# Four layers in one kernel: TensorE's work of a pair put in another order, SyncE's queries and masks issued first

## The chip, the cores and the metric

One core of a Trainium2 chip runs the whole program. The metric is device time in microseconds from launch to end. Three runs of the kernel before took 1097.38, 1100.94 and 1102.38 us. TensorE (PE) multiplies and transposes into PSUM, VectorE (DVE) and ScalarE (ACT) read PSUM and write SBUF, GpSimd (POOL) issues gathers, SyncE (SP) issues the other DMAs.

## The reference, cut to what matters

`x` is 64 sequences of 64 tokens of 512 values. Four layers, each added to its input:

```python
x = x + einsum('bct,bcd->bdt', x, W0[cond])                    # L0: a 64x64 matrix per sequence
q, k, v = x @ Wq.T, x @ Wk.T, x @ Wv.T                         # L1: 8 heads, 4 groups, 64 wide
q, k = rope(rms(q)), rope(rms(k))                              #     k, v scattered into 16-token blocks
p = softmax(where(allowed, q @ k_all.T / 16, -inf))            #     window of 256 keys before each token
x = x + (p @ v_all) @ Wo.T
x = x + einsum('bsi,bio->bso', x, W2[id]) + b2[id]             # L2: one of 16 experts (1 MB) per sequence
x = x + x @ W3.T + s * ((x @ A[ad].T) @ B[ad].T)               # L3: a shared matrix and a rank-16 adapter
```

## The kernel before

Two sequences make a pair: 128 tokens fill the 128 partitions, and there are 32 pairs. Stage A (the first 290 us or so) does L0, the projections, norm and rotation, and leaves x, queries and new keys and values in DRAM. Stage B, from about 290 us on, is what the change touches. Each engine runs its own instruction stream through the pairs: four written out, a loop of two pairs a turn, then the last ones. In turn `p` the attention of pair `p` runs, the output projection and the expert of pair `q = p - 1`, and the last layer of pair `r = p - 2`.

The attention of a pair has four steps `j`, two for each sequence, each with two units `u = 2j` and `2j + 1` that alternate between two buffers:
- GpSimd gathers 336 old rows of keys and values of a sequence into KV (`held`) and overwrites the new ones (`fresh`). `held(b)` of pair p waits until `values` of the same sequence of pair p - 2 is done (L1130).
- `keys` on TensorE turns the keys into bank 4 (L1418), ScalarE copies them to KT.
- `scores` (L1431): two products of 64 rows by 128 columns, one in each half of the array's rows, 336 columns each, into banks 0 and 1. They wait for KT, for the queries QB (first step), and for the earlier maxima `s_mx`, after which the banks are free.
- `masked` on VectorE (L1309) adds the mask FM and takes the maximum, `exp` on ScalarE (L1240) makes the probabilities and their sum, `norm` on VectorE (L1317, L1320) scales them.
- `turn` on TensorE (L1439) transposes them, `probs` on ScalarE copies them to PT, `values` on TensorE (L1452) multiplies them with the values: products 64 columns wide, one in each half of the array's columns, into bank 5. `heads` splits the result into high and low parts (OTH, OTL).

The rest of a turn: `output` (12 products over L93, the full array, bank 7), the sum x2 on VectorE (L1377), `turn_x(XB2)` (L1408), a copy to XT2, `expert` (L1477: 8 products of 64 columns, bank 6), the sum x3 (L1331), `turn_x(XB3)`, high and low parts XTH3 and XTL3, `adapter` (12 products of 128 columns), `dense3` (12 products of 512) and `adapted_sum`, and the last sum `out_sum` (L1337). Products in float32r are made exact by three (`exact_products`, L87 to L93), which is why each matrix comes as high and low.

Nothing plans the order: each `body` is written out by hand, with semaphores between engines, and an engine that waits holds all that stands behind. TensorE's is at L1523 to L1591, ScalarE's at L1254, VectorE's at L1339. SyncE's turn (L1184 to L1223) issues, in order: the expert weights of the first sequence (`weights(0)`, after `s_l2` of pair p - 2 and after the gather `held(1)` of pair p + 1 landed), the store of pair p - 2, x of pair p (after the sum x2 of pair p - 1), queries and masks of pair p + 1, the bias rows, and the weights of the second sequence (after `held(0)` of pair p + 2 landed).

Of the kernel before, what the change touches and what calls it, by code (L numbers as in the profile page):

```python
# [96 lines left out]
def build(nc, t, out):  # L97
    ctx = ExitStack()
    with ctx:
# [914 lines left out]
        with pb:  # L1014
# [148 lines left out]
            def _(sp):  # L1163
# [20 lines left out]
                def body(pr, attention, dense, adapted):  # L1184
# [22 lines left out]
                    if isinstance(p, int) and p == 0:  # L1207
                        sp.wait_ge(s_new[1], 16 * NCH)
                    if attention:
                        weights(0)  # L1210
# [6 lines left out]
                    if isinstance(p, int) and p == 0:  # L1217
                        sp.wait_ge(s_qto, 16 * PAIRS)
                    if not last_pair(pr):
                        queries(pr.move(1))  # L1220
                        windows(pr.move(1))
# [7 lines left out]
            def _(act):  # L1229
# [24 lines left out]
                def body(pr, attention, dense, adapted):  # L1254
                    p, q, r = pr.n, pr.n - 1, pr.n - 2
                    if adapted:
                        act.wait_ge(s_x3p, at(r, 1, 0))
                        copy(XTH3[:, :, :].rearrange("p k t -> p (k t)"), bank[7][:, :]).then_inc(s_xt3h, 1)
                    if dense:
                        probs(q, 6)  # L1260
                        probs(q, 7)
                    if attention:
                        exp(p, 0)
                        exp(p, 1)
                    if dense:
                        heads(q, 1)
                    if attention:
                        keys(pr, 1, 0)

                        probs(p, 0)  # L1270
                        probs(p, 1)
                        exp(p, 2)
                        exp(p, 3)

                        probs(p, 2)
                        probs(p, 3)
                        exp(p, 4)
                        exp(p, 5)
                        keys(pr, 1, 1)
                        heads(p, 0)  # L1280
                    if dense:
                        act.wait_ge(s_x2p, at(q, 1, 0))
                        copy(XT2[:, :, :, :].rearrange("p k b t -> p (k b t)"), bank[7][:, :]).then_inc(s_xt2, 1)

                    if attention:
                        probs(p, 4)
                        probs(p, 5)
                        exp(p, 6)
                        exp(p, 7)
                        if not last_pair(pr):  # L1290
                            keys(pr.move(1), 0, 0)
                            keys(pr.move(1), 0, 1)

                keys(Pair(0, 0), 0, 0)
                keys(Pair(0, 0), 0, 1)
# [3 lines left out]
            def _(dve):  # L1299
# [39 lines left out]
                def body(pr, attention, dense, adapted):  # L1339
# [23 lines left out]
                    if attention:  # L1363
                        masked(pr, 2)
                        masked(pr, 3)
                    if attention:
                        norm(p, 1)
                    if adapted and not last_dense(p):
                        out_sum(r, 6)
# [4 lines left out]
                    if dense:  # L1374
                        dve.wait_ge(s_o, at(q, 1, 0))
                        dve.wait_ge(s_x1in, at(q, 16, 15))
                        v.tensor_tensor(XB2[:, :], bank[7][:, :], XB1[:, :], ALU.add).then_inc(s_x2, 1)  # L1377
                    if attention:
                        norm(p, 2)
                        heads(p, 0)  # L1380
# [9 lines left out]
                    if attention:  # L1390
                        masked(pr, 6)
                        masked(pr, 7)
                        norm(p, 3)
                    if dense:
                        dve.wait_ge(s_xbb, at(q, 1, 0))
                        x3(q)

# [3 lines left out]
            def _(pe):  # L1401
# [10 lines left out]
                def keys(pr, b, gp):  # L1412

                    k = 2 * pr.par + b
                    if gp == 0:
# [106 lines left out]

                def body(pr, attention, dense, adapted):  # L1523
# [15 lines left out]
                    if attention:  # L1539
                        pe.wait_ge(s_kt, at(p, 4, 1))  # L1540
                        keys(pr, 1, 0)
                    if dense:
                        values(before, 3)
                    if adapted:
                        adapter(r, 7)
                        dense3(0, 2, True)

                    if attention:
                        scores(pr, 1)
                        turn(p, 0)  # L1550
                        turn(p, 1)
                    if adapted:
                        dense3(2, KC, False)
                        adapted_sum(r, 6)
                    if attention:
                        values(pr, 0)
                    if dense:
                        if adapted:
                            pe.wait_ge(s_xam, at(r, 1, 0))
                        output(q, 0, 2)  # L1560

                    if attention:
                        scores(pr, 2)
                        turn(p, 2)
                        turn(p, 3)
                    if dense:
                        output(q, 2, KC)
                    if attention:
                        values(pr, 1)
                        pe.wait_ge(s_kt, at(p, 4, 2))  # L1570
                        keys(pr, 1, 1)
                    if dense:
                        pe.wait_ge(s_x2, at(q, 1, 0))
                        turn_x(XB2, s_x2p)

# [4 lines left out]
                    if dense:  # L1580
                        expert(before, 0, 2)
                    if attention:
                        values(pr, 2)
                    if more:
                        pe.wait_ge(s_kt, at(p, 4, 3))
# [3 lines left out]
                    if more:  # L1589
                        pe.wait_ge(s_kt, at(p + 1, 4, 0))  # L1590
                        keys(pr.move(1), 0, 1)  # L1591

                keys(Pair(0, 0), 0, 0)
                pe.wait_ge(s_kt, 1)
                keys(Pair(0, 0), 0, 1)
# [51 lines left out]
```

## Time and profile before

| | |
|---|---|
| median of three runs | 1100.94 us |
| the profiled execution | 1101.85 us |
| its span, first to last instruction | 1100.0 us |
| mean granted TensorE clock | 0.984 |
| PE busy | 1031.8 us, 94% |
| DVE, ACT, POOL busy | 60%, 49%, 49% |
| DMA, mean over the span | 178 GB/s in packets |

In the timelines, "idle before" stands in brackets with what ended it. A row "x4" merges four instructions that lie together: its start is that of the first, its length reaches to the modelled end of the last. Matmuls are pipelined, so the step from one start to the next is what one costs, and is shorter than its length. PE and PEld are matmuls and weight loads; the sizes behind a tile's name, as 64*128, are the rows and columns of the array in use. In a row of sums (a stretch, its length, the busy time of PE, PEld, DVE, ACT and POOL with counts) the last three numbers are the granted clock, the DMA engines' share and GB/s.

### The profile page before, as it was taken

The numbers are of one execution on the slowest core, as the hardware profiler recorded it, in microseconds if no ns is written. First come the engines' busy times: TensorE is split into PE (matmuls) and PEld (weight loads), VectorE is DVE, ScalarE is ACT, GpSimd is POOL, SyncE is SP. The second block draws the span as 40 slices with busy tenths as digits, with TensorE's granted clock in tenths as the row PEclk, the third lists the DMA queues.
The fourth block names the chain that finished last, engine by engine and source line by source line (L and its number), as shares of the span: only waits on it lengthen the run. The fifth ranks groups of instructions, "written<-read, shape, count | busy, mean of one in ns | idle before, by whom it ended". The sixth has DMA issues, their size and how long they took to land.

```text
span 1100.0 us, 24023 instructions
## 1 busy us (share of the span) xinstructions
PE 1031.8 (94%) x6438; PEld 699.2 (64%) x6438; DVE 658.4 (60%) x1928; ACT 534.8 (49%) x1337; POOL 535.1 (49%) x597
## 2 busy tenths in 40 slices
PE   8999999999459999999999999999999999999998
PEld 6767777677336666666666666666666666666665
DVE  5889897567435555555555555555555555555552
ACT  4457776575344444444444444444444454444441
POOL 3555455257565455545544545555455545554400
PEclk9999999999689999999999999999999999999999
DMA  4433533454366666666666666666666666666631
GB/s 134 134 132 119 172 123 125 145 192 162 105 184 201 215 207 200 191 216 189 185 215 199 207 198 206 197 193 184 219 200 205 192 212 192 187 195 215 204 127 53
DMA packets 95337, 196.16 MB, mean 178 GB/s; under 512 B 31346, under 2 KB 40114, under 8 KB 87110
## 3 DMA queue, kind: packets, MB, share of 16 engines
q1 hardware_dynamic: 63942, 149.49, 41.7%
q0 software_dynamic: 30784, 44.16, 14.7%
q10 hardware_dynamic: 576, 2.10, 0.5%
q8 instruction: 15, 0.25, 0.1%
q14 instruction: 20, 0.16, 0.0%
HBM read 195.08 MB, written 33.56 MB: 208 GB/s over the span
## 4 chain that ended last, share of the span: by engine, by line
PE 64%; ACT 3%; issue 3%; DMA 2%; POOL 1%; ACTq 0%; DVE 0%; SPq 0%; POOLq 0%; DVEq 0%
PE bank L93 23%; PE bank L1477 10%; PE bank L1452 9%; PE bank L1431 9%; PE bank L1439 7%; PE bank L1418 4%; ACT PT L1231 2%; PE bank L1408 2%; DMA QB<-qt_scratch 2%; ACT KT L1231 1%; POOL KV L1132 0%; DMA KV<-in_pool,idxs 0%; POOL KVE L1142 0%; ACTq L76 0%; PE bank L1498 0%
## 5 line engine op out<-in xcount | busy, mean ns | idle before, releaser
L1231 ACT ACTIVATE PT<-bank 112x384 f32<-112x384 f32 x256 | 111.8, 489 | 263.2 <-PE bank L1439 263.0
L1309 DVE CUSTOM_DVE_ANT_0 SM<-bank,FM 128x336 f32<-128x336 f32 x256 | 129.8, 507 | 171.4 <-PE bank L1431 147.6
L1132 POOL DMA_INDIRECT KV<-in_pool,idxs x96 | 95.4, 993 | 116.5 <-PE bank L1452 94.9
L1132 POOL DMA_INDIRECT KVE<-in_pool,idxs_e x90 | 90.6, 1007 | 121.0 <-PE bank L1452 101.1
L1240 ACT ACTIVATE PR<-SM,nb 128x336 f32<-128x336 f32 x256 | 145.9, 577 | 1.7 <-DVE nb L1313 1.5
L1142 POOL DMA_INDIRECT KV<-kv_scratch,idxs x96 | 96.3, 1004 | 62.6 <-DMA KV<-in_pool,idxs 35.7
L1431 PE MATMUL bank<-KT,QB 64*128 64x336 f32 x512 | 108.9, 503 | 16.0 <-DMA QB<-qt_scratch 10.3
L1477 PE MATMUL bank<-W,XT 128*64 128x512 f32 x512 | 123.7, 604 | 0.0
L1142 POOL DMA_INDIRECT KVE<-kv_scratch,idxs_e x93 | 92.7, 997 | 62.7 <-DMA KVE<-in_pool,idxs_e 32.4
L1231 ACT ACTIVATE KT<-bank 128x336 f32<-128x336 f32 x128 | 57.5, 450 | 132.1 <-PE bank L1418 130.1
L93 PE MATMUL bank<-wqh,XTH 128*128 128x512 f32 x256 | 105.8, 413 | 9.6 <-DVE XTL L500 6.5
L1439 PEld LDWEIGHTS bank<-ident,PR 128*112 128x112 f32 x768 | 82.4, 134 | 46.3 <-issue 44.6
L1439 PE MATMUL bank<-ident,PR 128*112 128x128 f32 x768 | 110.7, 281 | 0.1
L93 PE MATMUL bank<-wqh,XTL 128*128 128x512 f32 x256 | 101.3, 396 | 0.0
L93 PE MATMUL bank<-wql,XTH 128*128 128x512 f32 x256 | 101.2, 395 | 0.0
L1320 DVE TENSOR_SCALAR PR<-PR,rinv 128x336 f32<-128x336 f32 x256 | 90.4, 395 | 4.5
L780 POOL TENSOR_TENSOR RT<-RT,SW 128x384 f32<-128x384 f32 x31 | 31.4, 1013 | 120.9 <-DVE SW L509 120.9
L1431 PEld LDWEIGHTS bank<-KT,QB 64*128 64x128 f32 x512 | 39.3, 187 | 51.0 <-issue 33.4
L93 PEld LDWEIGHTS bank<-wqh,XTH 128*128 128x128 f32 x256 | 48.7, 190 | 26.9 <-DVE XTL L500 13.9
L1331 DVE TENSOR_TENSOR XB<-bank,XBB 128x512 f32<-128x512 f32 x32 | 22.1, 692 | 71.9 <-PE bank L1477 71.9
L1452 PE MATMUL bank<-PT,KVE 112*64 112x128 f32 x768 | 55.8, 281 | 9.4 <-ACT PT L1231 9.4
L1317 DVE RECIPROCAL rinv<-rs 128x2 f32<-128x2 f32 x128 | 20.9, 163 | 72.1 <-ACT PR L1240 72.1
(195 smaller groups left out, 2175.0 us busy)
## 6 DMA issues: line engine op xcount, KB each, us to landing
W<-in_w SPq DMA_DIRECT2D x64, 1024.0 KB, 5.8
FM<-mask SPq DMA_DIRECT2D x64, 168.0 KB, 3.9
X<-in_x SPq DMA_DIRECT2D x32, 256.0 KB, 2.8
x_scratch<-X SPq DMA_DIRECT2D x32, 256.0 KB, 2.0
qt_scratch<-QT SPq DMA_DIRECT2D x32, 256.0 KB, 2.9
QB<-qt_scratch SPq DMA_DIRECT2D x32, 256.0 KB, 2.9
XB<-x_scratch SPq DMA_DIRECT2D x32, 256.0 KB
BB<-in_b SPq DMA_DIRECT2D x64, 128.0 KB
```

The source lines that it names most:

```text
L93: last = mm(out, l, r, start=start and i == 0, stop=stop and i == len(todo) - 1)
L1132: pool.indirect_dma_start(out=KV[k][:, c, :], out_offset=None, in_=t["pool"], in_offset=bass.IndirectOffsetOnAxis(ap=idxs[k][:, c:c + 1], ...
L1142: pool.indirect_dma_start(out=KV[k][:, c, :], out_offset=None, in_=kv_d, in_offset=bass.IndirectOffsetOnAxis(ap=idxs[k][:, NCH + c:NCH + c ...
L1231: return nc.scalar.activation(dst, src, ACT.Copy)
L1240: nc.scalar.activation(PR[u % 2][:, :], SM[u % 2][:, :], ACT.Exp, bias=nb[:, u:u + 1], scale=SCALE, accum_out=rs[:, u:u + 1]).then_inc(s_e, 1)
L1309: v.tensor_tensor_reduce(out=SM[u % 2][:, :], in0=bank[u % 2][:, 0:SPAN], in1=FM[k][:, :], scale=1.0, scalar=-3e38, op0=ALU.add, op1=ALU.m ...
L1320: v.tensor_scalar(PR[g2][:, :], PR[g2][:, :], rinv[:, 2 * j + g2:2 * j + g2 + 1], None, ALU.mult).then_inc(s_pn, 1)
L1418: last = nc.tensor.transpose(bank[4][:, c * CH:(c + 1) * CH], KV[k][:, c, gp * P:(gp + 1) * P], ident[0:CH, 0:CH])
L1431: mm(bank[g2][:, 0:SPAN], QB[pr.par][rows, b, 2 * gp:2 * gp + 2, :].rearrange("p c t -> p (c t)"), KT[b][rows, gp, :], start=True, stop=Tr ...
L1439: last = nc.tensor.transpose(bank[2 + u % 2][0:CH, c * P:(c + 1) * P], PR[u % 2][:, c * CH:(c + 1) * CH], ident[:, :])
L1452: last = mm(bank[5][g2 * HD:(g2 + 1) * HD, gp * P:(gp + 1) * P], KV[2 * pr.par + b][:, c, (G + g) * HD:(G + g + 1) * HD], PT[g2][:, c, :], ...
L1477: last = mm(bank[6][half * T:(half + 1) * T, :], XT2[:, k, half, :], W2[pr.par][half][:, k * D:(k + 1) * D], start=(k == 0), stop=(k == KC ...
```

## The change

On TensorE each of the four steps becomes: `scores`, then all full-array work, then the products of 64 columns. `keys` of a sequence moves one step later each (those of the first sequence's second half into the pair's own turn), with its wait inside `keys`. `dense3` is split by operand into `dense3_high` (the eight products with XTH3, which need only the high part) and `dense3_low`; `output` runs in one piece. `turn_x(XB2)` moves ahead of `turn(p, 2)`. ScalarE and VectorE follow: on ScalarE the copy of XT2 comes ahead of probs 2 and 3, on VectorE the sum x2 comes ahead of `masked` 4 and 5, `out_sum` ahead of norm 1, and x3 ahead of norm 3. On SyncE `queries` and `windows` of the next pair come first in a turn, ahead of `weights(0)`.

```diff
@@ -1206,6 +1206,11 @@
 
                     if isinstance(p, int) and p == 0:
                         sp.wait_ge(s_new[1], 16 * NCH)
+                    if isinstance(p, int) and p == 0:
+                        sp.wait_ge(s_qto, 16 * PAIRS)
+                    if attention and not last_pair(pr):
+                        queries(pr.move(1))
+                        windows(pr.move(1))
                     if attention:
                         weights(0)
                     if adapted:
@@ -1214,11 +1219,6 @@
                         return
                     wait(sp, s_x2, p)
                     sp.dma_start(XB1[:, :], x1_d[bass.ds(p, 1)]).then_inc(s_x1in, 16)
-                    if isinstance(p, int) and p == 0:
-                        sp.wait_ge(s_qto, 16 * PAIRS)
-                    if not last_pair(pr):
-                        queries(pr.move(1))
-                        windows(pr.move(1))
                     bias_rows()
                     weights(1)
 
@@ -1260,39 +1260,37 @@
                         probs(q, 6)
                         probs(q, 7)
                     if attention:
+                        keys(pr, 0, 1)
                         exp(p, 0)
                         exp(p, 1)
                     if dense:
                         heads(q, 1)
                     if attention:
-                        keys(pr, 1, 0)
-
                         probs(p, 0)
                         probs(p, 1)
+                        keys(pr, 1, 0)
                         exp(p, 2)
                         exp(p, 3)
-
-                        probs(p, 2)
-                        probs(p, 3)
-                        exp(p, 4)
-                        exp(p, 5)
-                        keys(pr, 1, 1)
-                        heads(p, 0)
                     if dense:
                         act.wait_ge(s_x2p, at(q, 1, 0))
                         copy(XT2[:, :, :, :].rearrange("p k b t -> p (k b t)"), bank[7][:, :]).then_inc(s_xt2, 1)
 
                     if attention:
+                        probs(p, 2)
+                        probs(p, 3)
+                        keys(pr, 1, 1)
+                        exp(p, 4)
+                        exp(p, 5)
+                        heads(p, 0)
+
                         probs(p, 4)
                         probs(p, 5)
+                        if not last_pair(pr):
+                            keys(pr.move(1), 0, 0)
                         exp(p, 6)
                         exp(p, 7)
-                        if not last_pair(pr):
-                            keys(pr.move(1), 0, 0)
-                            keys(pr.move(1), 0, 1)
 
                 keys(Pair(0, 0), 0, 0)
-                keys(Pair(0, 0), 0, 1)
                 bodies(act, body)
 
             @block.vector
@@ -1363,19 +1361,18 @@
                     if attention:
                         masked(pr, 2)
                         masked(pr, 3)
-                    if attention:
-                        norm(p, 1)
                     if adapted and not last_dense(p):
                         out_sum(r, 6)
-
-                    if attention:
-                        masked(pr, 4)
-                        masked(pr, 5)
+                    if attention:
+                        norm(p, 1)
                     if dense:
                         dve.wait_ge(s_o, at(q, 1, 0))
                         dve.wait_ge(s_x1in, at(q, 16, 15))
                         v.tensor_tensor(XB2[:, :], bank[7][:, :], XB1[:, :], ALU.add).then_inc(s_x2, 1)
-                    if attention:
+
+                    if attention:
+                        masked(pr, 4)
+                        masked(pr, 5)
                         norm(p, 2)
                         heads(p, 0)
                     if dense:
@@ -1390,10 +1387,11 @@
                     if attention:
                         masked(pr, 6)
                         masked(pr, 7)
-                        norm(p, 3)
                     if dense:
                         dve.wait_ge(s_xbb, at(q, 1, 0))
                         x3(q)
+                    if attention:
+                        norm(p, 3)
 
                 bodies(dve, body)
 
@@ -1412,6 +1410,7 @@
                 def keys(pr, b, gp):
 
                     k = 2 * pr.par + b
+                    wait(pe, s_kt, 4 * pr.n + 2 * b + gp)
                     if gp == 0:
                         pe.wait_ge(s_new[k], at(pr.i, 16 * NCH, 16 * NCH - 1))
                     for c in range(NCH):
@@ -1520,6 +1519,16 @@
                     exact_products(mm, bank[of][:, :], [(*x3t[k], w3_h[:, k, :], w3_l[:, k, :]) for k in range(a, b)],
                                    start, False)
 
+                def dense3_high(r):
+                    pe.wait_ge(s_xt3h, at(r, 1, 0))
+                    for k in range(KC):
+                        for w in (w3_h, w3_l):
+                            mm(bank[6][:, :], XTH3[:, k, :], w[:, k, :], start=k == 0 and w is w3_h, stop=False)
+
+                def dense3_low():
+                    for k in range(KC):
+                        mm(bank[6][:, :], XTL3[:, k, :], w3_h[:, k, :], start=False, stop=False)
+
                 def body(pr, attention, dense, adapted):
                     p, q, r = pr.n, pr.n - 1, pr.n - 2
                     before, more = pr.move(-1), attention and not last_pair(pr)
@@ -1537,62 +1546,54 @@
                         turn(q, 6)
                         turn(q, 7)
                     if attention:
-                        pe.wait_ge(s_kt, at(p, 4, 1))
-                        keys(pr, 1, 0)
+                        keys(pr, 0, 1)
+                    if adapted:
+                        dense3_high(r)
+                        adapter(r, 7)
                     if dense:
                         values(before, 3)
-                    if adapted:
-                        adapter(r, 7)
-                        dense3(0, 2, True)
 
                     if attention:
                         scores(pr, 1)
                         turn(p, 0)
                         turn(p, 1)
+                        keys(pr, 1, 0)
                     if adapted:
-                        dense3(2, KC, False)
+                        dense3_low()
                         adapted_sum(r, 6)
-                    if attention:
-                        values(pr, 0)
                     if dense:
                         if adapted:
                             pe.wait_ge(s_xam, at(r, 1, 0))
-                        output(q, 0, 2)
+                        output(q, 0, KC)
+                    if attention:
+                        values(pr, 0)
 
                     if attention:
                         scores(pr, 2)
-                        turn(p, 2)
-                        turn(p, 3)
-                    if dense:
-                        output(q, 2, KC)
-                    if attention:
-                        values(pr, 1)
-                        pe.wait_ge(s_kt, at(p, 4, 2))
-                        keys(pr, 1, 1)
                     if dense:
                         pe.wait_ge(s_x2, at(q, 1, 0))
                         turn_x(XB2, s_x2p)
+                    if attention:
+                        turn(p, 2)
+                        turn(p, 3)
+                        keys(pr, 1, 1)
+                    if dense:
+                        expert(before, 0, 2)
+                    if attention:
+                        values(pr, 1)
 
                     if attention:
                         scores(pr, 3)
                         turn(p, 4)
                         turn(p, 5)
-                    if dense:
-                        expert(before, 0, 2)
-                    if attention:
-                        values(pr, 2)
                     if more:
-                        pe.wait_ge(s_kt, at(p, 4, 3))
                         keys(pr.move(1), 0, 0)
                     if dense:
                         expert(before, 2, KC)
-                    if more:
-                        pe.wait_ge(s_kt, at(p + 1, 4, 0))
-                        keys(pr.move(1), 0, 1)
+                    if attention:
+                        values(pr, 2)
 
                 keys(Pair(0, 0), 0, 0)
-                pe.wait_ge(s_kt, 1)
-                keys(Pair(0, 0), 0, 1)
                 bodies(pe, body)
```

## Rows read from the trace of the kernel before

**Rows 1.** The page, its chain that ended last: shares of the span by engine.
```profile
PE 64%; ACT 3%; issue 3%; DMA 2%; POOL 1%; ACTq 0%; DVE 0%; SPq 0%; POOLq 0%; DVEq 0%
```

**Rows 2.** Waits, 520 to 1040 us: who <- for whom: us in total, times, longest.
```profile
PE bank L1452 <- ACT PT L1231: 10.6, 21, 0.5
PE bank L1431 <- ACT KT L1231: 3.7, 21, 0.2
```

**Rows 3.** Timeline, TensorE, 700 to 750 us: start, length, what, idle before.
```profile
709.13 0.65 PE L1408 MATMUL bank<-ident,XB 128*128 128x128 f32 x4
710.28 0.45 PE L1418 MATMUL bank<-ident,KV 112*128 112x112 f32 x3
711.24 0.88 PE L1452 MATMUL bank<-PT,KVE 112*64 112x128 f32 x12 [0.51 <-ACT PT L1231]
...
720.44 0.39 PE L93 MATMUL bank<-wll,OTH 128*128 128x512 f32 x1
720.67 0.40 PE L93 MATMUL bank<-wlh,OTL 128*128 128x512 f32 x1
721.00 0.83 PE L1431 MATMUL bank<-KT,QB 64*128 64x336 f32 x4
...
723.96 0.88 PE L1452 MATMUL bank<-PT,KV 112*64 112x128 f32 x12
724.77 0.51 PE L1418 MATMUL bank<-ident,KV 112*128 112x112 f32 x3
...
725.89 0.84 PE L1431 MATMUL bank<-KT,QB 64*128 64x336 f32 x4 [0.18 <-ACT KT L1231]
...
727.46 1.94 PE L1477 MATMUL bank<-W,XT 128*64 128x512 f32 x8
729.22 0.83 PE L1452 MATMUL bank<-PT,KV 112*64 112x128 f32 x12
729.98 0.51 PE L1418 MATMUL bank<-ident,KVE 112*128 112x112 f32 x3
730.42 1.94 PE L1477 MATMUL bank<-W,XT 128*64 128x512 f32 x8
732.29 0.51 PE L1418 MATMUL bank<-ident,KVE 112*128 112x112 f32 x3
```

**Rows 4.** Timeline, TensorE: scores(0) of pairs 2 and 31.
```profile
342.98 0.84 PE L1431 MATMUL bank<-KT,QB 64*128 64x336 f32 x4 [1.07 <-DMA QB<-qt_scratch]
...
1049.47 0.83 PE L1431 MATMUL bank<-KT,QB 64*128 64x336 f32 x4
```

**Rows 5.** Timeline, ScalarE and VectorE, in the pair of rows 3.
```profile
709.82 0.60 ACT L1231 ACTIVATE XTH<-bank 128x512 fp32r<-128x512 f32 x1 [0.90 <-PE bank L1408]
...
724.17 0.69 DVE L1377 TENSOR_TENSOR XB<-bank,XB 128x512 f32<-128x512 f32 x1 [0.56 <-PE bank L93]
```

**Rows 6.** Start of stage B: timeline, 310 to 320 us in sums, DMA issues.
```profile
298.07 0.79 PE L1418 MATMUL bank<-ident,KVE 112*128 112x112 f32 x3 [3.06 <-DMA KVE<-kv_scratch,idxs_e]
310.52 0.36 SPq L1197 DMA_DIRECT2D W<-in_w  x1
...
311.40 0.42 SPq L1166 DMA_DIRECT2D QB<-qt_scratch  x1
...
320.71 1.49 PE L1431 MATMUL bank<-KT,QB 64*128 64x336 f32 x4 [8.75 <-DMA QB<-qt_scratch]
...
322.65 10.38 SPq L1197 DMA_DIRECT2D W<-in_w  x2
...
310.00:320.00 10.00, 1.42 (x16) 0.82 (x12) 0.86 (x3) 1.58 (x6) 4.96 (x6) 0.75 0.86 258
...
W<-in_w SPq DMA_DIRECT2D x64, 1024.0 KB, 5.8
```

**Rows 7.** Timeline, SyncE's queue: expert weights of one turn.
```profile
733.76 10.05 SPq L1197 DMA_DIRECT2D W<-in_w  x2
```

## The prediction

> **What bounds the kernel now.** Read first the chain that ended last on the page [rows 1]: TensorE alone holds 64% of the span, and no other engine over 3%. Then the waits of 520 to 1040 us, 21.3 pairs in the middle of stage B [rows 2]: TensorE idles only twice in a pair, for PT ahead of `values` (10.6 us over 21 times) and for KT ahead of `scores` (3.7 us over 21). Last the timeline of one pair on TensorE [rows 3], where from one group's start to the next there is nearly always work. The pair's length comes from further apart: `scores(0)` of pair 2 starts at 342.98 and of pair 31 at 1049.47 [rows 4], 29 pairs, 24.36 us each. So a pair costs what TensorE's groups cost, plus two short stalls, plus what is lost where one kind of group follows another. That third part has to be read from the starts.
>
> **The two stalls.** The ten transposes of turn_x and turn from 709.13 to 710.28 take 1.15 us, 0.11 each and 0.05 for the change (below). `keys` at 710.28 is three shorter ones, 0.10 apart, and the next group would start about 0.19 behind the last, at 710.67; `values` starts at 711.24 [rows 3], so 0.57 us is lost. `scores` at 725.89 follows `keys` and turn_x from 724.77: 0.05 + 3 x 0.10 + 3 x 0.11 bring the last start to 725.45, and 0.20 to change over gives 725.65; lost 0.25 us. Together 0.82 us a pair (the waits view, which counts from modelled ends, shows 0.50 and 0.18 [rows 2]).
>
> **The price of changing the form.** The groups use the array in three forms: rows 64*128 (`scores`), columns *64 (`values`, `expert`), and the full array (everything else; the shapes stand in the rows). Leaving: two full-array matmuls of 512 columns start 0.23 us apart (720.44, 720.67), but the step to `scores` is 0.33 (721.00). The eight instructions of `expert` take 1.76 us when `values`, of the same form, follows (727.46 to 729.22) and 1.87 when `keys` follows (730.42 to 732.29). Either way leaving costs 0.10. Entering: `values` takes 0.81 us when it comes from full-array work (723.96 to 724.77) and 0.76 straight behind `expert` (729.22 to 729.98); so entering costs 0.05. A change of form costs 0.15 us. All in [rows 3].
>
> **Part 1, TensorE's order.** Per pair the old order changes form 18 times: three steps of scores / full / values / full make four each, and the last, with `keys` between the two halves of `expert`, makes six. The new order is scores, full, columns four times over: 12 changes. No matmul is added or removed (`dense3_high` and `dense3_low` are the twelve products of `dense3` regrouped). Six changes by 0.15 are 0.90 us. The change straight from columns to rows does not occur in a steady pair of the trace. Its bounds: nothing (4 x 0.15 less, period 22.05) and double (4 x 0.15 more, 23.25); I take 0.15, since leaving costs 0.10 in each of the three directions seen.
> The stall at `values(before, 3)` goes: `dense3_high` and `adapter` now stand ahead of it, and 8 x 0.23 + 12 x 0.11 = 3.2 us cover 0.57. The one at `scores(3)` goes because `expert` and `values(1)`, 2.5 us, now lie between `keys(1, 1)` and it. New period: 24.36 - 0.82 - 0.90 = 22.64 us.
>
> **What is late next.** I laid the new order out from `scores(0)` = 0 with the same steps, and asked of each group whether its input is there.
> (a) `dense3_high` is due at 0.77 (scores) + 0.49 (turn_x) + 0.66 (six turns) + 0.30 (keys) = 2.2. XTH3 is copied 0.69 us behind the start of turn_x (709.13 to 709.82) and takes 0.60 [rows 3, 5]: 0.77 + 0.69 + 0.60 = 2.06. Slack about 0.1 us, the smallest of all.
> (b) x2 now waits right behind `output`, with `masked(4)` and `masked(5)` queued behind it on VectorE. It started 0.54 us behind the last product of `output` (723.96 - 0.33 = 723.63, against 724.17) and takes 0.69 [rows 3, 5]. turn_x(XB2) needs it 1.3 us behind that product and is due 0.33 + 0.81 (values 0) + 0.77 (scores 2) = 1.9 behind it. Slack 0.6. Those masked rows belong to `scores(2)`, which itself starts only 1.1 us behind that product, so they lose nothing.
> (c) `expert` needs XT2: 0.69 + 0.60 = 1.29 behind the start of turn_x, due at 0.49 + 0.66 + 0.40 = 1.55. Slack 0.2 after a semaphore's 0.1.
> (d) ScalarE puts XT2 ahead of probs 2, 3 and the copy of `keys(1, 1)`, so exp 4 and 5 are later by 0.6; turn 4 comes 4.8 us behind turn_x's start, and XT2, two PT copies, KT, two exps, and the first scaling add to about 4.2. Slack 0.6.
> (e) x3 now stands ahead of norm 3 on VectorE. With `values(2)` and `scores(0)` (1.5 us) behind `expert`, norm 3 ends before turn_x(XB3) and its 0.49 us are over.
> None turns into a wait. If (a) and (c) miss by 0.2 us each, 29 pairs cost 12 us more.
>
> **Part 2, SyncE's order.** `queries` and `windows` issue three DMAs (256 and twice 168 KB) ahead of `weights(0)`, and are no longer behind the waits for `s_xo` and `s_x2`. Their own waits are for scores and maxima of the pair before the present one, long done. In a steady pair no one waited for QB or FM, so this is worth nothing there, and what is queued behind them (1 MB of W2) is needed a pair later. At the start of stage B it is worth much [rows 6]: QB of pair 1 was issued at 311.40, behind W2 at 310.52, and `scores` stood still for 8.75 us until 320.71. SyncE was held at `weights(0)` by gathers; the wait for `s_new[1]` ahead of it was over by 298.07, when `keys` read those rows. So QB and FM of pair 1 now go out near 298, and their cost of 8.75 us goes. What is late next is W2's second half for pair 0: issued at 322.65, 5.8 us to land, so 328.5. The burst ahead of it loses 0.6 MB; at the 258 GB/s that 310 to 320 us moved that is up to 2.3 us, so 326.1 to 328.5. From the first `expert` to pair 2's scores the new order has 1.76 + 0.76 + 0.77 + 0.66 + 0.40 + 1.77 + 0.75 = 6.9 us: pair 2 starts at 333.0 to 335.4 instead of 342.98. That gains 7.6 to 10.0; I take 8.8. If W2 takes the 9.3 us that QB took, it is 4 us.
>
> **The sum.** 29 pairs by 1.72 are 49.9 us [rows 4]. Start of stage B 8.8. Pair 31 (three changes fewer, the stalls) and the tail, where `dense3_high` fills the wait for XTL3: 1.5, between 0 and 3. Profiled execution 1101.85 - 60.2 = 1041.6. That execution is 0.9 above the median of 1100.94; I leave the forecast at 1041.6.
>
> **A rule to weigh.** The order of events at a change in [rows 3] is: last start, 0.1 us more than usual, next form. The Trainium skill (TensorEngine Tiling (Array Packing), Key Properties) says that changing the tiling mode, not just the tile, drains TensorE; the 1.76 against 1.87 us of `expert` agree. Against the change speaks TensorE: Matmul & The Clock Gate, Part 3, The mechanism, of the Trainium skill: a weight load overlaps running matmuls only when its row group differs. By that rule full-array groups would expose their loads whether together or apart, and the regrouping would save nothing: that is rival 2.
>
> **Rivals.**
> 1. A new short wait. (a) and (c) have 0.1 to 0.2 us, and pair times come from sums of rounded steps. Waits of 0.3 to 0.8 us a pair give 9 to 23 us: 1050 to 1065. Against: ScalarE is free ahead of both copies. Chance 0.20.
> 2. The loss at a change is that of any change of operand and stays. Then only the stalls go: 29 x 0.90 = 26 us more, 1068. Against: `values` behind `expert` changes operand too and paid nothing. Chance 0.07.
> 3. Columns to rows is free or nearly so: 29 x 0.60 = 17 us less, 1024 to 1030. Chance 0.08.
> 4. Start of stage B gives back nothing, since gathers and W2 set it: 1050. Inside the range. Chance 0.05, with the steady gain whole.
> 5. Slower: the W2 ring. `weights(1)` waits for the gather that `values(1)` sets free, and `expert`, ahead of the next `values(1)`, now waits for W2. `values` at 723.96 to W2's issue at 733.76 is 9.8 us [rows 3, 7], landing 5.8 [rows 6], `expert` 1.8: 17.4 us around. It decides above 22.6, and is slower than before by over 0.5% only above 24.55: gathers and W2 would have to take 7.2 us more in each pair. At 24.8 it would be 29 x 0.44 = 13 us more than before, with no gain at the start: 1115; from there down to 1107. For it: the ring ran later at the start of the stage (QB took 9.3 us). Against: the page's W2 median of 5.8. Chance 0.03.
> 6. It does nothing: the stalls come back elsewhere and the changes cost nothing. 1096 to 1106. Chance 0.03.
>
> **How the numbers follow.** The forecast holds 0.54, with 1033 to 1050 of its own. 1025 to 1062 takes in most of rivals 1 and 3 and all of 4. A measurement of this kernel can tell about 0.5% (5.5 us) from no change. Faster: 0.54 + 0.20 + 0.07 + 0.08 + 0.05 = 0.94; same 0.03; slower 0.03.
>
> **What would show it.** `scores(0)` to `scores(0)` at 22.6 us; a step of 0.33 where columns meet `scores`, with no idle time ahead of `values(3)`, `dense3_high` or `expert`; QB of pair 1 issued near 298 and no wait of `scores` for it; pair 2's scores at 333 to 335, with the wait on W2 just before. A period over 23 us with an idle row for XTH or XT is rival 1; without an idle row, but with 0.33 steps inside full-array work, rival 2.

## The result, and the profile after

The changed kernel takes 1040.56 us (median of 4 runs, 1037.87 to 1041.41) against 1100.12 before: ratio 0.945, 95% interval 0.9431 to 0.9469. The profiled execution is 1041.25 us long with a span of 1039.4. Of the twelve runs below, e5 to e12 ran on another chip than e1 to e4, where the kernel before itself took 1151 and 1157 us. (The expectations of e10 to e12 speak of another chip than before; it was the one of e5 to e9 again.) Their traces hold idle times of VectorE and ScalarE, most of 1 to 6 us and up to 8.0, for nothing the profile names. They are read by the pairs and steps without such a stretch, and by their ratio to the kernel before beside them. One of e7's six runs took 1617.39 us at a granted clock of 0.557 and is in its median, but in no ratio.

One pair of the changed kernel on TensorE, from its timelines (start, length, line, shapes, count; the pair from `scores(0)` at 652.43 to the next at 674.98):

```profile
652.43 0.84 PE L1430 MATMUL bank<-KT,QB 64*128 64x336 f32 x4
653.20 0.65 PE L1406 MATMUL bank<-ident,XB 128*128 128x128 f32 x4
...
654.57 0.47 PE L1526 MATMUL bank<-wlh,XTH 128*128 128x512 f32 x1
...
657.87 0.88 PE L1451 MATMUL bank<-PT,KV 112*64 112x128 f32 x12
658.68 0.83 PE L1430 MATMUL bank<-KT,QB 64*128 64x336 f32 x4
...
664.97 0.88 PE L1451 MATMUL bank<-PT,KVE 112*64 112x128 f32 x12
665.78 0.83 PE L1430 MATMUL bank<-KT,QB 64*128 64x336 f32 x4
...
669.84 0.83 PE L1451 MATMUL bank<-PT,KVE 112*64 112x128 f32 x12
670.60 0.84 PE L1430 MATMUL bank<-KT,QB 64*128 64x336 f32 x4
671.37 0.87 PE L1438 MATMUL bank<-ident,PR 128*112 128x128 f32 x6
...
674.22 0.83 PE L1451 MATMUL bank<-PT,KVE 112*64 112x128 f32 x12
674.98 0.84 PE L1430 MATMUL bank<-KT,QB 64*128 64x336 f32 x4
```

22.55 us where [rows 4] gave 24.36. No row carries an idle time: the waits view of 520 to 1000 us has no row for TensorE, where that of the kernel before had the two of [rows 2]. The new junction, columns to rows, stands four times: `values` takes 0.81 us from full-array work into `scores` (657.87, 664.97) and 0.76 behind `expert` (669.84, 674.22). These are the steps that `values` took into full-array work in [rows 3]; so columns to rows costs what columns to full costs. `dense3_high` starts 1.37 us behind turn_x (653.20 to 654.57).

The start of stage B, TensorE and SyncE's queue, and sums over 5 us (stretch, length, busy PE, PEld, DVE, ACT, POOL, granted clock, DMA share, GB/s), against [rows 6]:

```profile
297.33 0.35 SPq L1166 DMA_DIRECT2D QB<-qt_scratch  x1
...
310.09 0.84 PE L1430 MATMUL bank<-KT,QB 64*128 64x336 f32 x4
...
320.02 0.79 PE L1417 MATMUL bank<-ident,KV 112*128 112x112 f32 x3 [4.08 <-DMA KV<-kv_scratch,idxs]
...
321.07 0.63 PE L93 MATMUL bank<-wll,OTH 128*128 128x512 f32 x1
321.49 0.63 PE L93 MATMUL bank<-wlh,OTL 128*128 128x512 f32 x1
...
328.61 1.94 PE L1476 MATMUL bank<-W,XT 128*64 128x512 f32 x8
...
335.51 0.83 PE L1430 MATMUL bank<-KT,QB 64*128 64x336 f32 x4
...
322.52 0.36 SPq L1197 DMA_DIRECT2D W<-in_w  x1
...
320.00:325.00 5.00, 4.98 (x14) 4.03 (x15) 0.92 (x3) 1.56 (x5) 2.69 (x3) 0.50 0.32 81
```

QB of pair 1 goes out at 297.33, pair 1 starts at 310.09 instead of 320.71. But then its `keys(1, 0)` waits 4.08 us for gathered rows, and behind the pause TensorE runs at half its clock (0.50, 1.2 GHz) for 5 us: `output` has its products 0.42 us apart instead of 0.23. Pair 2 starts at 335.51 instead of 342.98.

The start differs from one execution to the next. e4 (below) has the changed kernel's start, since its edit acts from pair 2 on. Its profile shows at the same two places (TensorE's timeline and the sums over 5 us):

```profile
317.69 0.48 PE L1417 MATMUL bank<-ident,KV 112*128 112x112 f32 x3 [1.80 <-DMA KV<-kv_scratch,idxs]
...
326.08 1.50 PE L1476 MATMUL bank<-W,XT 128*64 128x512 f32 x5 [0.99 <-DMA W<-in_w]
...
320.00:325.00 5.00, 5.00 (x36) 2.97 (x34) 2.74 (x9) 1.81 (x5) 3.78 (x5) 1.00 0.72 212
```

There the gather came sooner, the clock stayed at 1.00, `expert` waited 0.99 us for W2, and pair 2 started at 332.98: 40.2 us behind `scores(0)` of pair 0, against 42.5 in the changed kernel's profile and 49.5 before. So 7.5 us below is what one execution gained, and the next can gain 2 us more.

The sum against the forecast, between the two profiled executions:

| | forecast | measured |
|---|---|---|
| pairs 2 to 30, 29 periods | 49.9 | 51.4 (706.49 less 655.07) |
| start of stage B, pair 2's scores | 8.8 | 7.5 (0.5 of it lies ahead of stage B) |
| pair 31 and tail | 1.5 | 1.7 |
| all | 60.2 | 60.6 |

### The profile page after: what moved, and what is told of

It reads as the page before. It is cut to its first block, busy times and chain, and to the rows that moved or that the text cites. A ratio compares the mean times of both kernels' runs of the same rounds, so it can differ in the third digit from the quotient of the medians.

```text
span 1039.4 us, 24011 instructions
## 1 busy us (share of the span) xinstructions
PE 999.3 (96%) x6438; PEld 714.5 (69%) x6438; DVE 659.8 (63%) x1928; ACT 537.5 (52%) x1337; POOL 543.0 (52%) x597
## 4 chain that ended last, share of the span: by engine, by line
PE 62%; DMA 5%; issue 3%; POOL 2%; POOLq 0%; DVE 0%; ACT 0%; DVEq 0%; ACTq 0%
PE bank L93 14%; PE bank L1476 10%; PE bank L1430 8%; PE bank L1451 8%; PE bank L1438 8%; PE bank L1526 5%; PE bank L1406 3%; PE bank L1417 3%; DMA KVE<-in_pool,idxs_e 3%; PE bank L1530 3%; DMA KV<-in_pool,idxs 1%; DMA KVE<-kv_scratch,idxs_e 1%; POOL KVE L1142 1%; POOL KV L1142 0%; POOL KV L1132 0%
## 5 line engine op out<-in xcount | busy, mean ns | idle before, releaser
L1132 POOL DMA_INDIRECT KV<-in_pool,idxs x96 | 98.2, 1023 | 44.4 <-issue 26.7
L1318 DVE TENSOR_SCALAR PR<-PR,rinv 128x336 f32<-128x336 f32 x256 | 93.7, 408 | 4.5
L1231 ACT ACTIVATE XT<-bank 128x512 f32<-128x512 f32 x32 | 19.1, 598 | 145.8 <-PE bank L1406 145.8
L1231 ACT ACTIVATE OTH<-bank 128x256 fp32r<-128x256 f32 x64 | 24.6, 384 | 87.2 <-PE bank L1451 87.2
L1231 ACT ACTIVATE KT<-bank 128x336 f32<-128x336 f32 x128 | 58.8, 460 | 13.5 <-PE bank L1417 13.3
L1476 PEld LDWEIGHTS bank<-W,XT 128*64 128x64 f32 x512 | 31.3, 136 | 46.9 <-issue 37.7
```

The source lines that it names most:

```text
L1132: pool.indirect_dma_start(out=KV[k][:, c, :], out_offset=None, in_=t["pool"], in_offset=bass.IndirectOffsetOnAxis(ap=idxs[k][:, c:c + 1], ...
L1231: return nc.scalar.activation(dst, src, ACT.Copy)
L1318: v.tensor_scalar(PR[g2][:, :], PR[g2][:, :], rinv[:, 2 * j + g2:2 * j + g2 + 1], None, ALU.mult).then_inc(s_pn, 1)
L1476: last = mm(bank[6][half * T:(half + 1) * T, :], XT2[:, k, half, :], W2[pr.par][half][:, k * D:(k + 1) * D], start=(k == 0), stop=(k == KC ...
```

## Experiments

The edits are shown cut to the calls that move.

**The two parts apart.** e1 is the changed kernel with SyncE's turn as before, e2 the kernel before with SyncE's new turn.

```diff
 e1: -  queries(pr.move(1)); windows(pr.move(1))      # ahead of weights(0)
     +  queries(pr.move(1)); windows(pr.move(1))      # behind XB1's DMA
 e2: the same in reverse, on the kernel before
```

> The changed kernel with SyncE's turn as it was before; TensorE, ScalarE and VectorE changed. My theory (the two parts are separate, SyncE's order matters only at the start of stage B): scores(0) to scores(0) stays at 22.55 us; pair 1 waits about 10 us for QB again, and pair 2 starts at 340 to 342 instead of 335.5, so 1046 to 1047 us. Rival (the queries' place matters in each pair, since it moves W2's issue): period 22.7 or more, over 1051 us.

> The kernel before with SyncE's new turn alone. My theory: steady period 24.36 us unchanged; pair 1 starts near 312, but the gather that keys(1, 0) of pair 1 needs lands near 320 and stands ahead of scores(1) in the old order, so that pair 2 starts only 4 to 5 us sooner than 342.98: 1095 to 1097 us. Rival (the start's gain of 7.5 us belongs to SyncE alone): pair 2 at 335.5, 1093 us.

e1: 1061.57 us, ratio 0.9643 (0.9621 to 0.9666). e2: 1100.41 us, ratio 1.0001 (0.9986 to 1.0016). In e1 my theory fell; in e2 the late gather was where I put it, but the gain of 4 to 5 us was not there. In e1 most pairs take 22.55 us, but eleven of 29 take 22.8 to 25.3 and a `scores` waits for QB. The waits view of e1, 520 to 950 us (us in total, times, longest), and its timeline around one such wait; behind it SyncE's queue in the kernel before, in the pair that began at 732.72, and a row of its waits (`--engine SP`, 700 to 800 us):

```profile
PE bank L1430 <- DMA QB<-qt_scratch: 8.0, 7, 1.9
```

```profile
726.69 0.33 SPq L1197 DMA_DIRECT2D W<-in_w  x1
...
727.77 0.34 SPq L1216 DMA_DIRECT2D XB<-x_scratch  x1
728.37 0.79 SPq L1166 DMA_DIRECT2D QB<-qt_scratch  x1
...
737.05 0.83 PE L1430 MATMUL bank<-KT,QB 64*128 64x336 f32 x4 [0.91 <-DMA QB<-qt_scratch]
```

```profile
743.48 0.33 SPq L1197 DMA_DIRECT2D W<-in_w  x1
...
749.41 0.34 SPq L1216 DMA_DIRECT2D XB<-x_scratch  x1
750.01 0.33 SPq L1166 DMA_DIRECT2D QB<-qt_scratch  x1
...
SPq L1216 <- DVE XB L1377: 22.5, 5, 4.5
```

In e1 SyncE leaves `weights(0)` at 727.0, 13.5 us into the pair that began at 713.53. QB goes out at 14.8 (728.37), 1.7 us behind 1 MB of W2, and is there only 8.7 us later, while the pair leaves it 7.7. In the kernel before, QB had no more room: it went out 17.2 us into a pair and had 7.1. But there SyncE stood for 4.5 us a pair at the wait for x2 (the last row), between W2 and QB, so QB followed W2 by 6.2 us or more and landed in 2.6 to 3.9 us in the 14 steady pairs from 4 on whose landing the trace holds. The new order has x2 ready sooner (e1's waits have no such row), and QB lands in W2's wake: in the ten pairs where `scores` waited, it took 7.6 to 9.4 us. So the rival was right that the queries' place matters in each pair, and with its number, over 1051 us. Its reason, that W2's issue moves, is not what shows: e1 has no wait for W2. What in W2's wake holds QB, its place in a queue or the bandwidth, no run here separates. Of the 21 us between e1 and the changed kernel, 12.3 lie in pairs 2 to 30 (667.3 against 655.1 us; 11.2 are waits for QB) and 8.1 at pair 2's start (343.58 against 335.51; 1.6 of them ahead of stage B).

e2's pair 2 starts at 340.37; its stage B began 1.8 us sooner, so the order gained 0.8. In the old order `keys(1, 0)` stands ahead of `scores(1)`, and there it waits for the same gather:

```profile
311.92 0.84 PE L1431 MATMUL bank<-KT,QB 64*128 64x336 f32 x4
318.71 0.79 PE L1418 MATMUL bank<-ident,KV 112*128 112x112 f32 x3 [5.16 <-DMA KV<-kv_scratch,idxs]
320.91 1.49 PE L1431 MATMUL bank<-KT,QB 64*128 64x336 f32 x4
```

Neither part gives the start's gain alone: in e2 8.75 us of waiting for QB are exchanged for the gather, since `scores(1)` and `turn` do not stand ahead of that `keys`.

**The price of a change of form.** e3 puts `keys` between `expert` and `values(2)`, e4 puts `dense3_low` between `values(3)` and `scores(1)`.

```diff
 e3:   turn(p, 4); turn(p, 5)
     - keys(next, 0, 0); expert(before, 2, KC); values(pr, 2)
     + expert(before, 2, KC); keys(next, 0, 0); values(pr, 2)
 e4: - values(before, 3); scores(pr, 1); turn 0, 1; keys(pr, 1, 0); dense3_low()
     + values(before, 3); dense3_low(); scores(pr, 1); turn 0, 1; keys(pr, 1, 0)
```

> The changed kernel with keys(next, 0, 0) between expert(2, KC) and values(2) instead of ahead of expert: the same groups, but the array changes form twice more in a pair (columns, full, columns). Price of a change of form 0.15 us: period 22.85 us, 9 us more in all, 1049 to 1050. Rival (the loss belongs to any change of operand, and there are as many groups as before): period 22.55, 1040 to 1041.

> The changed kernel with dense3_low moved behind values(3), so that columns to rows becomes columns, full, rows at one of the four places. If columns to rows costs as much as the other changes: 0.15 us a pair more, period 22.70, 1045. If columns to rows is free: 0.30 more, 22.85, 1049. If it costs double: nothing more, 22.55.

e3: 1059.52 us, ratio 0.9628 (0.9604 to 0.9653), 23.18 and 23.26 us a pair in turn, 0.67 more than the changed kernel on average and over twice what I expected. The timeline says where:

```profile
608.68 0.86 PE L1438 MATMUL bank<-ident,PR 128*112 128x128 f32 x6
609.48 1.94 PE L1476 MATMUL bank<-W,XT 128*64 128x512 f32 x8
611.35 0.51 PE L1417 MATMUL bank<-ident,KVE 112*128 112x112 f32 x3
611.78 0.88 PE L1451 MATMUL bank<-PT,KV 112*64 112x128 f32 x12
612.59 0.83 PE L1430 MATMUL bank<-KT,QB 64*128 64x336 f32 x4
613.36 0.66 PE L1406 MATMUL bank<-ident,XB 128*128 128x128 f32 x4
614.22 0.86 PE L1438 MATMUL bank<-ident,PR 128*112 128x128 f32 x6 [0.21 <-DVE PR L1318]
```

From turn 4 to the next `scores` are 3.91 us (608.68 to 612.59) against 3.61 in the changed kernel (671.37 to 674.98), with the same groups: 0.30 for two changes, as priced. The rest, 0.37, is a wait: turn_x to turn takes 0.86 us instead of 0.49. The copy of the late `keys` on ScalarE stands ahead of exp 6 and 7, and norm 3 follows them. The rival that any change of operand costs the same is out.

e4: 1045.26 us, ratio 0.949 (0.9466 to 0.9515). Its four runs (1043.39 to 1045.53) all lie above the changed kernel's (1037.87 to 1041.41), though the two ratios' intervals touch, and 27 of its pairs take 22.75 or 22.76 us where those took 22.54 or 22.55. One change more costs 0.21 us. Its rows:

```profile
658.73 0.88 PE L1451 MATMUL bank<-PT,KV 112*64 112x128 f32 x12
659.53 1.21 PE L1530 MATMUL bank<-wlh,XTL 128*128 128x512 f32 x4
660.67 0.83 PE L1430 MATMUL bank<-KT,QB 64*128 64x336 f32 x4
```

`values` takes 0.80 us as into `scores`; the four products take 1.14, against 4 x 0.23 within full-array work. Of the 0.21 more, 0.10 is for leaving and 0.11, not 0.05, for entering. With 0.15 for the change into `scores` both changes are 0.36, so e4 would cost 0.36 more if columns to rows were free and 0.06 if it were double; 0.21 puts it at 0.15.

**What covers a stall.** e5 and e10 (the same kernel) put `values(3)` ahead of `dense3_high` and `adapter` again. e6 is the kernel before with `values(3)` moved behind `adapter` and `dense3(0, 2)`. e8 and e11 (the same kernel) move `keys(0, 1)` behind `dense3_high`.

```diff
 e5, e10: - keys(pr, 0, 1); dense3_high(r); adapter(r, 7); values(before, 3)
          + keys(pr, 0, 1); values(before, 3); dense3_high(r); adapter(r, 7)
 e6:      - values(before, 3); adapter(r, 7); dense3(0, 2, True)
          + adapter(r, 7); dense3(0, 2, True); values(before, 3)
 e8, e11: - keys(pr, 0, 1); dense3_high(r); adapter(r, 7)
          + dense3_high(r); keys(pr, 0, 1); adapter(r, 7)
```

> The changed kernel with values(3) of the pair before ahead of dense3_high and adapter again. My theory: values(3) is due 2.3 us behind scores(0) and the second PT copy ends at 2.9, so a wait of 0.6 us comes back, and one change of form more costs 0.15: period 23.3 us, 22 us more in all, 1062 to 1064. Rival (the wait was no loss, another place takes it up later in the pair): period 22.7, 1045.

> values(3) ahead of dense3_high and adapter, on another chip than before (there all kernels, the kernel before too, showed scattered stalls of 1 to 3 us in most pairs; the fastest pair took 23.31 us). My theory: 23.3 us in every pair, 1062 to 1064 us. Rival (another place takes the wait up): 22.7, 1045.

e5: 1167.63 us, ratio 1.0183 (1.0113 to 1.0253); e10: 1181.34 us, ratio 1.0217 (1.0162 to 1.0272): slower than the kernel before beside them, by about 2%. In 46 of the 50 pairs from 7 on, `scores(0)` to `scores(1)` takes 7.00 to 7.02 us against 6.24 in the changed kernel: 0.77 more, where 0.75 was expected, with the wait in its place (e10, 520 to 1000 us):

```profile
PE bank L1451 <- ACT PT L1231: 8.0, 16, 0.5
```

That would be 23.3 us a pair, which e5's fastest pair took. About half of the pairs took 27 to 28, from the stalls of VectorE and ScalarE named above. Why this order is hit by them so much harder than the others stays open, so the 22 us in all that I expected are shown by the step and not by the time.

> The kernel before with values(3) moved behind adapter and dense3(0, 2), and nothing else. If any full-array work in front of values(3) gives the stall back, 0.57 + 0.15 us a pair are saved: period 23.64, 1079 us. My theory says the cover must itself be ready: adapter needs XTL3, which VectorE ended 0.9 us behind adapter's new due time, so a wait of about 1.0 us on XTL3 takes the place of the 0.57 on PT: period 24.6, 1106 to 1110 us.

e6: 1209.43 us, ratio 1.0488 (1.0415 to 1.0561). The sign is as expected, the size is not to be had from this run, since its later steps are disturbed. The first step takes 7.00 us in its undisturbed pairs, against 6.60 before, and the waits of 430 to 1150 us name XTL:

```profile
PE bank L93 <- DVE XTL L1303: 29.1, 22, 2.0
```

So 2.7 us of work ahead of `values(3)` do not serve if they have to wait themselves; cutting `dense3` by operand is what made the cover.

> The changed kernel with keys(0, 1) behind dense3_high instead of ahead of it, so that dense3_high is due 0.30 us sooner. My estimate was a slack of 0.1 us there: then a wait of 0.2 us for XTH3 appears in each pair, period 22.75, 1046 us. If the slack is larger than 0.3: period 22.55, 1040 to 1041.

> keys(0, 1) behind dense3_high, on another chip than before (there the fastest pairs took 22.83 us). With a slack of 0.1 us at XTH3: period 22.75 to 22.85, 1046 to 1049 us. With a slack over 0.3: 22.55, 1040 to 1041.

e8: 1107.45 us, ratio 0.9633 (0.9574 to 0.9693); e11: 1121.56 us, ratio 0.968 (0.9621 to 0.974). The first step takes 6.54 to 6.57 us in undisturbed pairs, 0.30 more, and the fastest pairs 22.83 and 22.88. In e8's timeline:

```profile
1009.49 0.66 PE L1406 MATMUL bank<-ident,XB 128*128 128x128 f32 x4
1009.98 0.82 PE L1438 MATMUL bank<-ident,PR 128*112 128x128 f32 x6
1010.84 0.51 PE L1526 MATMUL bank<-wlh,XTH 128*128 128x512 f32 x1
```

`dense3_high` starts 1.35 us behind turn_x, 1.34 in the other undisturbed pairs: that is when XTH3 is there. The changed kernel starts it 1.37 behind. The slack was 0.02 to 0.03 us, not 0.1: a copy of XTH3 that came later than that would have shown in every pair.

**The start of stage B.** e7 and e12 (the same kernel) let `weights(0)` of pair 0 go without the wait for the gather of pair 1; e9 adds a wait for pair 1's fresh rows.

```diff
   def weights(b):        # for p == 0 and b == 0 alone
 e7, e12: - landed(b)
 e9:      + sp.wait_ge(s_new[3], 16 * NCH)
```

> The changed kernel; for pair 0 alone weights(0) does not wait for the gather of pair 1, so that 1 MB of W2 goes out near 300 us instead of 310.6. If W2 in the burst of 310 to 320 us is what held the gather that keys(1, 0) of pair 1 waited for (4.1 us, and then half clock for 5 us): keys starts near 316 to 317, pair 2 at 329 to 333 instead of 335.5, 1036 to 1038 us. If the gathers are held by their own issue on GpSimd: pair 2 within 1 us of 335.5, 1040 to 1041.

> W2's first half for pair 0 near 300 us, on another chip than before. If W2 beside the gathers delays them: the gather held(1) of pair 1 lands later than 310.5, its fresh rows later than 320, and pair 2 starts at 336 us or later: 1041 to 1045. If moving 1 MB out of the burst at 310 helps more: pair 2 at 329 to 333, 1036 to 1038.

> The changed kernel; for pair 0 alone weights(0) waits in addition until the fresh rows of pair 1's second sequence have landed, so that the 1 MB of W2 does not run beside them (the run that sent it out earlier, at 301.7 us, had the gathers later, not sooner). If W2 beside the gathers is what held keys(1, 0) of pair 1 for 4.1 us: that wait and the half clock behind it go, expert of pair 0 then waits for W2's second half until about 324.5, and pair 2 starts near 331.5 instead of 335.5: 1036 to 1038 us. If the gathers are slow by themselves: keys again near 320, W2 later, pair 2 at 336 to 340, 1041 to 1045.

e7: 1100.97 us, ratio 0.9539 (0.9481 to 0.9598); e12: 1119.86, 0.9675 (0.9624 to 0.9727); e9: 1118.09, 0.9681 (0.9632 to 0.973). For the start compare from `scores(0)` of pair 0 to that of pair 2: 52.7 us in e7, 50.5 in e12, 47.5 in e9; 45.4 in e8 and 48.6 in e11, whose start is the changed kernel's, on the same ground; 42.5 in the changed kernel. With W2 out near 300 us, the gather that was issued meanwhile came later (GpSimd's queue in e12, and the same row in e7):

```profile
307.38 0.20 POOL L1115 COPY idxs_e<-idxT 112x6 int32<-112x6 int32 x1
312.42 1.01 POOL L1142 DMA_INDIRECT KV<-kv_scratch,idxs  x1 [4.83 <-DMA KV<-in_pool,idxs]
...
314.27 1.01 POOL L1142 DMA_INDIRECT KV<-kv_scratch,idxs  x1 [5.33 <-DMA KV<-in_pool,idxs]
```

In e11 the same instruction went out at 308.99, 0.40 us behind the copy, and within 0.5 us in the changed kernel, e3, e4, e8 and e9 too. So 1 MB of W2 beside a gather (with the 0.5 MB of x and bias rows that follow it in SyncE's queue) holds the gather, by 4.4 us in e12. Moving W2 moves the wait: the next gather's, of 4.95 us in the changed kernel with W2 out at 310.63, is 0.22 in e12 and 0.47 in e7.

e9 does not settle its question. With W2 at 313.49 behind the gathers `keys(1, 0)` had no wait, but neither had it in e8 and e11, where pauses of 7.64 and 6.60 us held TensorE ahead of it; in e9 such pauses were 3.09 and 1.93 us. Then `expert` waited 2.85 us, for the copy of XT2, which itself stood behind an idle time of ScalarE with no engine of this core named:

```profile
330.31 0.60 ACT L1233 ACTIVATE XT<-bank 128x512 f32<-128x512 f32 x1 [6.36 <-remote]
```

No arrangement was seen to bring pair 2 forward; whether one without the pauses would, stays open. No version here beats the changed kernel.

## Why the prediction was right, and where it was not

- **The stalls.** 0.82 us a pair, both gone. e5 and e10 give the first back at 0.77 with a change of form, as its term says; by the new order's steps 0.75 was due. Right.
- **The price of changes.** 0.15 each, 0.90 a pair. e3 shows 0.30 for two. Stalls and changes together were to make 22.64; measured 22.55. Of the missing 0.09, 0.06 can be read in the kernel before: there `output` is entered from columns, and its second product starts 0.34 us behind the first instead of 0.23, so entering cost 0.11 and not 0.05. The new order enters no such run from columns.

```profile
718.60 0.88 PE L1452 MATMUL bank<-PT,KV 112*64 112x128 f32 x12
719.40 0.50 PE L93 MATMUL bank<-wlh,OTH 128*128 128x512 f32 x1
719.74 0.39 PE L93 MATMUL bank<-wll,OTH 128*128 128x512 f32 x1
```

  What leaving `scores` itself costs can't be read, but both orders do it four times a pair.
- **Columns to rows.** Taken as 0.15 between nothing and double; the rows of the changed kernel and e4 agree.
- **The tight places.** (a) held, with 0.02 to 0.03 us instead of 0.1; e8 shows that a slack of less would have been rival 1. (b) to (e) held. The layout by hand was right to about 0.1 us, which is as fine as its smallest slack; that rival 1 did not come about was in part luck.
- **29 equal pairs.** Pairs 3 and 4 took 23.42 and 22.95 us. In pair 3 `expert` took 2.64 us instead of 1.77, its last product starting at 375.94 behind W2's second half, issued at 367.75. This is rival 5's ring, at the start alone, 1.3 us in all.
- **SyncE in a steady pair.** "This is worth nothing there" was wrong for the change as a whole: it is worth 12 us under the new order (e1), and nothing under the old (e2). The step that failed read from "no one waited for QB" in the old order that QB's place would not matter in the new one. What kept QB quick was the wait for x2 that held it 6 us behind W2; part 1 takes that wait away, and in W2's wake QB takes 8.7 us instead of some 3, with 7.7 left (e1). With queries first, QB goes out 4 to 10 us into most pairs and has over 12. The sum did not suffer, since both parts came together; that was luck, for the prediction gave no reason why part 1 would need part 2.
- **The start.** 8.8 taken, 7.5 measured, and the late one named wrongly: W2's second half, issued at 322.52 as foreseen, was in time; the gather for `keys(1, 0)` was late, 4.08 us, and half clock after it cost some 2 us more (ten products 0.2 us later each). The prediction had no row for that gather's landing. That `expert` still started at 328.61, next to the 326.1 to 328.5 forecast for W2, is luck in this execution: a wait left out and a wait that was not there came to the same. In e4's execution W2 was the last to come, as forecast, and pair 2 started at 332.98, as forecast. The terms' errors (1.5 more in the pairs, 1.3 less at the start, 0.2 more in the tail) partly cancel in the total.

## What to carry to other kernels

On an engine that bounds the kernel, count how often neighbouring groups change the array's form and put groups of one form together; read the price from two neighbours that differ in form and two that don't. Cover a wait with work whose own input is already there, if need be by cutting that work by operand. And when a reordering makes an input ready sooner, ask each in-order queue again what now follows what: a wait that goes away can put a small urgent transfer right behind a large one. A change worth nothing by itself can carry a third of another one's gain.

## What the runs showed of the hardware

- A change of form costs 0.10 us leaving and 0.05 entering with transposes or 64-column products; entering a run of 512-column float32r products from columns costs 0.11 (kernel before: 0.34 us between its first two products, 0.23 between the next; e4: 1.14 us for four that take 0.93, with 0.10 for leaving). e3 adds two changes and 0.30 us.
- 256 KB of QB issued 1.4 to 2.6 us behind 1 MB of W2 took 7.6 to 9.4 us in the ten pairs of e1 that waited for it; issued 6.2 to 7.1 us behind, it took 2.6 to 3.9 in the kernel before.
- Behind a gather issued 3 to 7 us after 1 MB of W2, GpSimd's next one had to wait 4.83 and 5.33 us (e12, e7); without W2 beside it, at most 0.5.
- TensorE's granted clock was 0.50 in the 5 us behind an idle time of 4.1 us (315 to 320 us: 0.81), and products of 512 columns were 0.42 to 0.43 us apart instead of 0.23. In e4, behind an idle time of 1.80 us at the same place, it stayed at 1.00.
- In e10, VectorE and ScalarE, which had stood still for 4.60 and 5.06 us, started again at the same time, with no engine of this core named as the one they waited for:

```profile
889.07 0.29 DVE L1353 TENSOR_TENSOR XAM<-bank,adapt 128x128 f32<-128x128 f32 x1 [4.60 <-remote]
889.07 0.87 ACT L1231 ACTIVATE PT<-bank 112x384 f32<-112x384 f32 x2 [5.06 <-remote]
```

  XAM's own input, the last product of `adapter`, had started at 884.65. What they waited for the profile does not show.
